# First keys of the next batch turned in visits 17 to 20, projections two per visit; half of the second attention's key norms as c'Gc in two passes

## The reference, cut to what matters

```python
# layer 0: heads of 16; keys and queries are layer-normed per head
kv = (y_main @ [Wk Wv] + b).reshape(b, s2, H, 32)      # 1585 rows; 16 more rows have weights of their own
k = _ln(kv[..., :16], kn_w, kn_b);  v = kv[..., 16:]
ctx = softmax(q k' / 4) v + the same over the 16 other rows

# layer 1: heads of 128; keys and queries are divided by their root mean square
q = rmsnorm((x @ Wq).reshape(b, 256, H, 128), gq)
k = rmsnorm((c @ Wk).reshape(b, 1601, H, 128), gk)      # c is the context
out = softmax(q k' / sqrt(128)) (c @ Wv) @ Wo
```

## Time and profile before

| | |
|---|---|
| median of 3 runs | 1887.56 us (1885.32 to 1890.52) |
| the profiled execution's own time | 1886.42 us |
| its span, first to last instruction | 1884.6 us |
| TensorE busy | 1798.2 us (95%) |
| VectorE, ScalarE, GpSimd busy | 1412.9 (75%), 1217.1 (65%), 351.4 (19%) |
| mean granted TensorE clock | 0.984 |
| first attention | about 52 to 390 us |
| key stages of the second | about 55 us each, from 636.8, 870.6, ... |

### The profile page before, as it was taken

How to read it: one execution, slowest core, us unless ns; L and a number is a source line. 1 busy time by engine, 2 the same in 40 slices (tenths; PEclk the granted TensorE clock), 3 DMA queues, 4 the chain that set the end, 5 groups by cost and what they waited for, 6 DMA issues and landing times.

```text
span 1884.6 us, 31894 instructions
## 1 busy us (share of the span) xinstructions
PE 1798.2 (95%) x9292; PEld 1330.8 (71%) x9292; DVE 1412.9 (75%) x2328; ACT 1217.1 (65%) x2056; POOL 351.4 (19%) x309
## 2 busy tenths in 40 slices
PE   5789898999999999999999999999999999999998
PEld 3444444568888777787777767777777777888887
DVE  7555656556666889897898988989789997666665
ACT  4566666852222778886888867888788885222222
POOL 3010101204544400001000010000100102444442
PEclk9899999989999999999999999999999999999999
DMA  3414131345443200001000010000000000544552
GB/s 98 110 27 101 48 80 45 83 163 131 109 111 89 71 1 1 0 0 36 1 1 0 0 35 1 1 0 0 1 23 1 0 17 18 114 111 105 115 115 74
DMA packets 109735, 95.90 MB, mean 51 GB/s; under 512 B 72820, under 2 KB 94200, under 8 KB 109016
## 3 DMA queue, kind: packets, MB, share of 16 engines
q1 hardware_dynamic: 109656, 94.88, 20.3%
HBM read 72.94 MB, written 1.44 MB: 39 GB/s over the span
## 4 chain that ended last, share of the span: by engine, by line
PE 83%; DVE 9%; ACT 2%; issue 2%; SPq 1%; POOL 1%; DMA 1%; DVEq 0%; ACTq 0%
PE ps L1347 36%; PE ps L474 17%; PE ps L486 8%; PE ps L1192 5%; PE ps L1179 4%; PE ps L1363 3%; PE ps L1117 3%; PE ps L1428 1%; SPq L583 1%; PE ps L1371 1%; PE ps L1456 1%; DVE s_rk L2055 1%; POOL s_p L825 1%; ACT s_p L1056 1%; DVE s_dsum L2131 1%
## 5 line engine op out<-in xcount | busy, mean ns | idle before, releaser
L1056 ACT ACTIVATE s_p<-ps,s_g,s_rk 128x256 f32<-128x256 f32 (+1 forms) x832 | 413.2, 561 | 8.6 <-DVE s_dsum L2131 8.2
L1347 PE MATMUL ps<-s_qq,s_ctxT 128*128 (+3 forms) x1248 | 357.0, 399 | 6.6 <-ACT s_p L1056 5.9
L474 PE MATMUL ps<-s_xT,s_wgus 128*128 128x512 f32 x1440 | 350.1, 392 | 0.0
L1347 PE MATMUL ps<-s_ps,s_ctx 128*128 128x512 f32 x1152 | 324.5, 395 | 0.9 <-DVE s_ps L2122 0.9
L474 PEld LDWEIGHTS ps<-s_xT,s_wgus 128*128 128x128 f32 x1440 | 270.9, 189 | 59.7 <-issue 1.5
L2122 DVE TENSOR_TENSOR s_ps<-s_p,s_ps 128x512 fp32r<-128x512 f32 x384 | 269.2, 701 | 20.7 <-ACT s_ps L1064 17.3
L931 ACT ACTIVATE s_p<-ps,s_bsm 128x1024 f32<-128x1024 f32 x208 | 219.7, 1112 | 95.3 <-PE ps L1192 85.0
L1347 PEld LDWEIGHTS ps<-s_qq,s_ctxT 128*128 128x128 f32 (+1 forms) x1248 | 222.8, 184 | 68.6 <-ACT s_p L1056 11.3
L1347 PEld LDWEIGHTS ps<-s_ps,s_ctx 128*128 128x128 f32 x1152 | 215.6, 188 | 56.2 <-DVE s_ps L2122 4.2
L2131 DVE TENSOR_TENSOR s_dsum<-s_dsum,s_p 128x512 f32<-128x512 f32 (+1 forms) x352 | 242.0, 687 | 16.3 <-ACT s_p L1056 12.4
L1926 DVE TENSOR_TENSOR s_hs<-s_hw,s_hs 128x512 fp32r<-128x512 f32 x120 | 141.4, 1178 | 80.6 <-ACT s_hs L385 80.6
(11 more groups left out here) (270 smaller groups left out, 2049.6 us busy)
## 6 DMA issues: line engine op xcount, KB each, us to landing
s_wB<-w1s SPq DMA_DIRECT2D x64, 256.0 KB, 3.8
s_kT<-s_kst SPq DMA_DIRECT2D x96, 128.0 KB, 2.4
s_kT<-s_kst SPq DMA_DIRECT2D x96, 80.0 KB, 2.1
s_wB<-w0s SPq DMA_DIRECT2D x15, 384.0 KB, 3.6
s_wB<-w0s SPq DMA_DIRECT2D x16, 256.0 KB, 3.8
s_wgu<-in_L_ffn_Wg_dram SPq DMA_DIRECT2D x64, 64.0 KB, 2.8
s_wgu<-in_L_ffn_Wu_dram SPq DMA_DIRECT2D x64, 64.0 KB, 2.6
s_wd<-in_L_ffn_Wd_dram SPq DMA_DIRECT2D x64, 64.0 KB, 2.4
```

The source lines that it names most:

```text
L474: ins = nc.tensor.matmul(ps[:, 4 + g, :], WGUS[f][:, slot, w, g, k, :], XT[f][:, x_, k, n], start=c == 0, stop=c == len(ops) - 1)
L1056: ins = nc.scalar.activation(p1[0:r, SLOT1[t], j, :], ps[0:r, BANK1[t], j * SQ:(j + 1) * SQ], ACT.Exp, bias=g1[0:r, 3:4], scale=rk_col(t, ...
L1347: ins = nc.tensor.matmul(out, lhs(x_), rhs(y_), start=first and n == 0, stop=last and n == 2)
```

## The change

In the first attention the projections stand in the free places of visits 4 to 11 (first and second places of visits 4, 5, 6, 9 and 10, the first of 7, 8 and 11), the keys in the first places of visits 17 to 20, squares and root move forward, and the second side job runs behind the values of the visit's first step. In the second, two of the four quarters (26 of 52 tiles) are norms by c'Gc: G is made once from Wk on TensorE and split; a tile is c G in two passes (high part of c alone), ScalarE copies it out, GpSimd multiplies it by c + low(c), and VectorE sums it three tiles later. `KINDS` interleaves the kinds; each has a ring of its own (3 and 4 slots). Taking the turned queries from PSUM moves from VectorE to ScalarE.

```diff
-KSQ = 7
+KSQ = (3, 4)
+GRAM = (1, 3)
+KINDS = "kkgkgkkkkggkkgggggggggggggkkkkggkkgkkkggkkkgkgkgkkgk"
+WEIGH_LAG = 3
+NORM_BEHIND = (1, 20)
+SCALE_AT, TURN_AT, TAKE_AT = (4, 6), (15, 22), (12, 20)
+KEY_AT, HIGH_AT, LOW_AT, NEXT_AT = 17, 14, 14, 20
...
-        first.update({4 + t: ("proj", b + 1, t) for t in range(KT)})
-        first.update({20: ("keys", b + 1, 0, 0), 21: ("query", b + 1, 0), 22: ("keys", b + 1, 0, 3)})
-        second.update({20: ("keys", b + 1, 0, 1), 21: ("keys", b + 1, 0, 2)})
+        places = [(work, u) for u in range(4, 12) for work in (first, second) if u not in work]
+        for t, (work, u) in enumerate(places[:KT]):
+            work[u] = ("proj", b + 1, t)
+        first.update({17 + c: ("keys", b + 1, 0, c) for c in range(4)})
+        first[21] = ("query", b + 1, 0)
...
-SQUARE = (18, 27, 35, 37)
-ROOT = 40
+SQUARE = (15, 21, 25, 28)
+ROOT = 32
...
@@ TensorE, a visit @@
-                    prepare(second)
                     if tiles == 3:
                         scores_at(n + 5)
-                    for k in range(tiles):
+                    values(b, step)
+                    prepare(second)
+                    for k in range(1, tiles):
                         values(b, step + k)
...
@@ TensorE, between the first queries @@
+                    if b == 0 and j in (1, 2):
+                        pe.wait_ge(s.m1_low, 4)
+                        for h in range(4):
+                            w = wkT1[:, 4 * GRAM[j - 1] + h, :]
+                            ins = nc.tensor.matmul(ps[:, 1 + j, h * P:(h + 1) * P], w, w, start=True, stop=True)
+                        ins.then_inc(s.gram_made, 1)
...
@@ TensorE, a tile @@
+                    if kind == "k":
+                        product(out, ctx_cols(u), w).then_inc(s.k1_made, 1)
+                    else:
+                        for part in range(2):
+                            ins = nc.tensor.matmul(out, ctx_cols(u)(0), w(part), start=part == 0, stop=part == 1)
+                        ins.then_inc(s.k1_made, 1)
...
@@ ScalarE, a tile @@
+                        if i >= KSQ[1]:
+                            act.wait_ge(s.gram_reduced, i + 1 - KSQ[1])
+                        nc.scalar.copy(lengths(kind, i, u), ps[0:ROWS1[u], n % 4, :]).then_inc(s.k1_squared, 1)
...
@@ GpSimd, a batch, behind the making of c + low(c) @@
+                for half, m, q, u, n, kind, i in key_tiles(b):
+                    if kind == "k":
+                        continue
+                    if weighed in NORM_BEHIND:
+                        norm_queries(TB * b + NORM_BEHIND.index(weighed))
+                    weighed += 1
+                    pool.wait_ge(s.k1_squared, n + 1)
+                    k = lengths(kind, i, u).rearrange("p (h d) -> p h d", h=4)
+                    g_.tensor_tensor(k, k, st[0:ROWS1[u], u, :].unsqueeze(1).to_broadcast([ROWS1[u], 4, C]), ALU.mult).then_inc(s.k1_weighed, 1)
...
@@ VectorE, a tile @@
+                    if kind == "k":
+                        reduce(kind, i, q, u, n)
+                    back = 2 * KT * half + m - WEIGH_LAG
+                    if back >= 0 and tiles[back][5] == "g":
+                        _, _, q, u, n, kind, i = tiles[back]
+                        reduce(kind, i, q, u, n)
...
@@ SyncE, ahead of loading the next batch's context rows @@
+                    sp.wait_ge(s.k1_weighed, 2 * KT * b)
```

226 lines of the change are left out of this document (133 added, 93 removed).

## The result

The change is worth 15.1 us: the median of four runs is 1871.30 us (1869.66 to 1871.98), that of the kernel before, on the same chip, 1886.44 us (1884.46 to 1890.52); the ratio is 0.9916, with a 95% interval from 0.9903 to 0.9929. Forecast were 38.1 us less, 1848.3 us, with a range from 1834 to 1869. The sign was right, the size was not.

The account below looks back on a forecast made before the run. TensorE was taken to bound both changed stages. First attention 18.3 us, key stages 3 x 6.0 and batch 0's 1.8 sum to 38.1 less than 1886.42: 1848.3 us, range 1834 to 1869.

Parts of the forecast that it names:

- A projection costs TensorE 0.84 us, wherever it stands: First attention: a visit with a projection takes 2.98 us against 2.14 without, so each projection costs 0.84 us.
- Built anew from prices: 63.4: First attention, visits 4 to 23: steps, projections and turns sum to 63.4 us; with waits 71.2 against 76.5.
- the gain in visits 20 to 23: First attention: nine steps and five turns take 16.0 us, by prices 11.9, once VectorE's query reads leave the key turns.
- Next visits 0 and 2 ... 0.8 a batch: First attention, next batch's visits 0 and 2: second job behind one step's values covers most of a wait, 0.8 us a batch.
- rival 1: The first attention gives nothing, as VectorE's waits among paired projections eat the gain: 1866.6 us, chance 0.13.
- 26 tiles x 0.232 = 6.0 us a batch; it counts in full only if nothing is later than TensorE at the end.: Second attention's key stage: one pass fewer in 26 tiles saves TensorE 6.0 us a batch, if no engine ends later.
- with 6.0 less, the variance is due at 918.1: Key stage's end: the variance of the norms, at 924.12 us before, comes 6.0 us sooner, still 1.9 behind TensorE's last tile.
- has 15 us free: Key stage: ScalarE can take over the queries' scaling from VectorE, as it has 15 us free.
- Rival 2: The key stage gives nothing, as smaller rings and a three-tile lag bring VectorE's waits for GpSimd to TensorE: 1868.1, chance 0.12.
- The low part of m1 ... I take nothing, and 4.6 us once as the bad end: Batch 0: m1's low part, moved ahead beside the normalizing, costs nothing, at worst 4.6 us once.
- the 1.8 of its sum: Batch 0's key stage: 6.0 us won, less 1.7 for making G and 2.5 for later queries, leaves 1.8.
- Rival 3: Slower: GpSimd's multiplies bound the key stage, at 1.88 us each 1899.7 us; or they exclude VectorE's sums; chance of either 0.06.

Follow-up runs that it names:

- e12: The changed kernel with four edits (1855.75 us), but a visit's second projection too stands ahead of all its values, so none are cut: 1859.81 us.
- e3: The changed kernel (1871.30 us), but a second side job stands behind one step's values only where it is a projection; sums and queries stand ahead: 1866.38 us.
- e5: The changed kernel (1871.30 us), but in batch 2 VectorE makes the turned context's low part ahead of the update of x: 1869.91 us.
- e4: The changed kernel (1871.30 us), but GpSimd makes m1's low part behind the turning of the normalized input, not beside the normalizing: 1864.90 us.

## Why the prediction was wrong

**"A projection costs TensorE 0.84 us, wherever it stands"** failed. It is 1.02 for each in a visit with two (1.13 for the second in e12, where no values are cut), and ten of the 13 stand in such visits: 1.8 us more. The price came from the visits with one. **"Built anew from prices: 63.4"** failed with it, and could have been doubted from its own rows: TensorE was busy 69.00 us in that stretch, 5.6 more than the prices give. To it come five turns in cut values at 0.28 us (e3), 1.4, and a three-step visit takes 3.46 us, not 3 x 1.07, 1.0 for the four of them. With the 4.4 of waits that is 63.4 + 1.8 + 1.4 + 1.0 + 4.4 = 72.0 of the measured 73.5; 1.5 us are not accounted for. What held was where the waits are, and the gain in visits 20 to 23: 10.7 us for 16.0 before, under the 11.9 of the prices. It was lost in visits 4 to 19, 62.8 us for 60.3. What failed was TensorE's own work.

**"Next visits 0 and 2 ... 0.8 a batch", and silence on the last batch.** The order within a visit was weighed only where it covers a wait. It also acts where there is none: 1.5 us lost in the last batch (e3). This was in the diff to be read, since the edit is not under `more`. So the first attention gave 8.5 in the profile, 10.6 alone, for 18.3: rival 1 was half true.

**"26 tiles x 0.232 = 6.0 us a batch; it counts in full only if nothing is later than TensorE at the end."** The price was right (5.8), and the condition was named. What failed is the step behind it, "with 6.0 less, the variance is due at 918.1": it kept the lag of 1.9 us, and so took the other engines as free. The lag is 2.98 us, and the variance came 4.7, 4.4 and 3.9 us nearer to the stage's start in batches 1, 3 and 2. The prediction put the queries' scaling (the takings of turned queries) on ScalarE because it "has 15 us free"; that is its busy share of the whole stage, and in the last 3 us no pause of it is listed. There two of those takings (0.68 and 0.70 us) stand between the last squares: 0.77 of the 1.10 us; the other 0.33 is VectorE's one sum more. VectorE was not free either: in the kernel before no pause of it is listed in the 20.7 us before the variance, and its last sum was the later one. Rival 2 named rings and lag, not this. How the gain came about: the sum of the second queries' squares starts 28.4 us in the stage for 32.8, by the 14 two-pass tiles ahead of those queries (14 x 0.232 = 3.2) and two tiles fewer ahead of them (1.4). The two-pass tiles behind them gain too, as they keep TensorE's last tile from being 2.1 us later. What a shorter row of VectorE alone, or of ScalarE alone, would give there is at most the 0.13 us by which they differ in this trace.

That the stretches behind the batches gave 12.4 of 18.0 is in part luck: 1.6 us of batch 1's 6.3 are the clock of the kernel before.

**Batch 2** gave 1.7 us of its 6.0: 3.9 won in the stage, 2.2 lost ahead of it, where TensorE waited 4.08 us for the context's low part, and had waited 1.92 before. The prediction left out the work that stands ahead of that part on VectorE; e5 shows 4.2 us in that place.

**"The low part of m1 ... I take nothing, and 4.6 us once as the bad end"**: worse than the bad end came. The wait is 4.25 us, the lower clock behind it costs about 2.7 more, and 1.6 come back in the stage: 5.3 us (e4). The prediction had a row of a VectorE instruction held by GpSimd and used it for L2032, but did not ask which VectorE work the moved 4.6 us would now stand beside. The Trainium skill's page "SBUF — State Buffer", section "SBUF: two separate sides", counts the two-port forms of VectorE among those that exclude GpSimd; by that rule the normalizing would be held, and the rows (6.88 for 2.67 us, e4) agree. With m1 behind, batch 0 gives 2.0 us for the 1.8 of its sum. That is agreement of the sum, and its terms were not tested one by one: L2110, the instruction on one column that was put at 3.4 us, takes 2.23 in e4 and 0.94 in the changed kernel.

**Rival 3** is refuted in both its ways. The multiply takes 1.09 us, under the taken 1.27 and far from the 1.75 at which it would turn to a loss, and sums beside multiplies keep 676 ns. The row was the better guide there than a rule stretched to all of VectorE.

**Nothing was forecast for the pair loops**, which the change does not touch: +3.5 us in the profile, most of it with the clock, lower behind a gap that grew from 0.72 to 1.36 us. Of the 23.7 us between forecast and profile, 9.8 are the first attention, 5.6 the key stages, 5.1 the start of the second attention, 3.5 the pair loops, less 0.3 at the ends.

## What to carry to other kernels

Matmuls saved are time saved only as far as the other engines' work at the end of the stage lets them. Before a lag is carried over, read the last few microseconds of every engine there, pauses too short for the listing included, and ask what the change puts between those instructions; time that an engine has free elsewhere in the stage does not help. When a GpSimd instruction with SBUF inputs is moved, look at each VectorE instruction that it will newly stand beside, once for every batch that differs from the others. A wait can cost more than itself: here a lower clock stood behind one of 4.25 us. A price from one form of a loop body holds for that form, and an edit to an order acts also in the iterations that have none of the work it was meant for.
